# Attention with four PSUM banks for the turned scores, two for the row scores, and the value products between the two row-unit slots of a quad

## The reference, cut to what matters

```python
x = x + _L1_attn_ref(_layernorm(x, axis=-1), ...)
# in _L1_attn_ref: NH, NKV = 32, 8 heads of HD = 16, causal, rotary positions
q = _apply_rope(q, cos, sin)
k = _apply_rope(k, cos, sin)
logits = jnp.einsum('bhqd,bhkd->bhqk', q, k) * scale
logits = jnp.where(causal[None, None], logits, jnp.finfo(logits.dtype).min)
attn = jax.nn.softmax(logits, axis=-1)
out = jnp.einsum('bhqk,bhkd->bhqd', attn, v)
return out.transpose(0, 2, 1, 3).reshape(bsz, q_len, NH * HD) @ Wo.T
```

## Time and profile before

| | us |
|---|---|
| runs shown | 2533.43, 5908.05, 2530.44; median 2533.43 |
| the profiled execution, its own time | 2539.86 |
| its span | 2538.0 |
| granted TensorE clock, mean over the span | 0.958 |

### The profile page before, as it was taken

The page is one execution under the profiler, slowest core; times in us unless marked ns, Lnnn a source line. Parts: engine busy times, 40 slices in busy tenths (PEclk is TensorE's granted clock), DMA queues, the critical chain, the costliest instruction groups (busy, mean ns, idle before and its releaser), DMA issues. The chain is left out here.

```text
span 2538.0 us, 33152 instructions
## 1 busy us (share of the span) xinstructions
PE 2358.7 (93%) x12442; PEld 1812.6 (71%) x12442; DVE 1660.0 (65%) x2163; ACT 1311.4 (52%) x1905; POOL 1330.1 (52%) x876
## 2 busy tenths in 40 slices
PE   6997899999999999999999999999889977877876
PEld 5875788888888888888888888887668744554433
DVE  6555787687687588588588588678365345664414
ACT  3214576577477477477477467567323132234423
POOL 2221498598599499499489589579422200000000
PEclk9998899999999999999999999999889988869988
DMA  5321333233233233233223333232143202000001
GB/s 134 96 73 54 107 113 104 87 110 103 86 102 117 79 112 113 79 108 108 88 92 117 90 102 112 88 100 84 42 116 88 65 14 79 1 2 1 3 1 47
DMA packets 163406, 204.07 MB, mean 80 GB/s; under 512 B 24396, under 2 KB 86224, under 8 KB 163120
## 3 DMA queue, kind: packets, MB, share of 16 engines
q1 hardware_dynamic: 163248, 201.96, 26.5%
HBM read 198.43 MB, written 3.15 MB: 79 GB/s over the span
## 5 line engine op out<-in xcount | busy, mean ns | idle before, releaser
L1914 POOL TENSOR_TENSOR mamba_w_lo<-mamba_raw,mamba_w_hi 128x512 fp32r<-128x512 f32 x272 | 435.8, 1611 | 292.0 <-ACT mamba_w_hi L1742 292.0
L76 PE MATMUL psum<-mamba_hT_lo,mamba_w_hi 128*128 128x512 f32 x1152 | 461.9, 401 | 3.0 <-DVE mamba_bc L2005 3.0
L78 PE MATMUL psum<-mamba_hT_hi,mamba_w_lo 128*128 128x512 f32 x1152 | 456.3, 396 | 0.0
L77 PE MATMUL psum<-mamba_hT_hi,mamba_w_hi 128*128 128x512 f32 x1152 | 456.1, 396 | 0.0
L1933 POOL TENSOR_SCALAR mamba_L<-mamba_A,mamba_ts 128x256 f32<-128x256 f32 (+1 forms) x256 | 335.0, 1322 | 0.1
L2037 DVE TENSOR_TENSOR mamba_L<-mamba_L,mamba_cb 128x1536 f32<-128x1536 f32 x128 | 302.8, 2366 | 22.8 <-ACT mamba_L L1791 14.3
L2005 DVE SCALAR_TENSOR_TENSOR mamba_hid<-psum,mamba_cw,mamba_hid 128x1022 f32<-128x1022 f32 (+2 forms) x192 | 245.1, 1277 | 19.4 <-ACT mamba_hid L1749 14.8
L76 PEld LDWEIGHTS psum<-mamba_hT_lo,mamba_w_hi 128*128 128x128 f32 x1152 | 217.0, 188 | 53.2 <-DVE mamba_bc L2005 3.3
L78 PEld LDWEIGHTS psum<-mamba_hT_hi,mamba_w_lo 128*128 128x128 f32 x1152 | 216.7, 188 | 52.4
L77 PEld LDWEIGHTS psum<-mamba_hT_hi,mamba_w_hi 128*128 128x128 f32 x1152 | 217.1, 188 | 49.1
L2064 DVE SCALAR_TENSOR_TENSOR mamba_zs_lo<-mamba_z,mamba_dgn,mamba_zs_hi 128x512 fp32r<-128x512 f32 x128 | 117.4, 922 | 172.2 <-ACT mamba_zs_hi L1814 172.2
(11 more groups left out here) (281 smaller groups left out, 4945.7 us busy)
## 6 DMA issues: line engine op xcount, KB each, us to landing
mamba_A<-mamba_a_dram SPq DMA_DIRECT2D x128, 512.0 KB, 4.5
mamba_raw<-in_win SPq DMA_DIRECT2D x144, 256.0 KB, 2.6
mamba_raw<-in_wout SPq DMA_DIRECT2D x128, 256.0 KB, 2.6
mamba_Eb<-mamba_e_dram SPq DMA_DIRECT2D x128, 128.0 KB, 3.0
ffn_raw<-in_w SPq DMA_DIRECT2D x80, 128.0 KB, 3.6
ffn_scl<-in_s SPq DMA_DIRECT2D x80, 128.0 KB, 3.7
ffn_scl<-in_s SPq DMA_DIRECT2D x86, 64.0 KB, 2.3
ffn_raw<-in_w SPq DMA_DIRECT2D x20, 256.0 KB, 2.6
```

What stands on the lines that cost most here:

```text
L76: e.matmul(out, wh, ml, start=start, stop=False)
L77: e.matmul(out, wh, mh, start=False, stop=False)
L78: return e.matmul(out, wl, mh, start=False, stop=stop)
L1914: e.tensor_tensor(w.lo[:, k % NSPLIT, :], raw[:, k % NRAW, :], w.hi_read[:, k % NSPLIT, :], ALU.subtract).then_inc(s["w_lo"], 1)
```

## The change

Three things change. Turned scores get four banks, 2 to 5: half m = 0 uses 2 and 3, half m = 1 uses 4 and 5, and `score_t` waits for the exponentials of the half before the last. Row units get one pair, banks 0 and 1: each waits until the reduction of the unit before it is done. And the value products of the quad before move from the end of a quad to its middle, behind the first half's row units and ahead of the second half's `score_t`.

```diff
                 def score(s, z):
                     b, qt = STEPS[s]
                     k, n = s * NQ + z, P * (qt + 1)
-                    if k >= 2:
-                        e.wait_ge(peaked, k - 1)
+                    if k:
+                        e.wait_ge(peaked, k)
                     for h in range(2):
-                        e.matmul(psum[:, 2 * (k % 2) + h, 0:n], qs[HALVES[h], b, z, qt * P:(qt + 1) * P],
+                        e.matmul(psum[:, h, 0:n], qs[HALVES[h], b, z, qt * P:(qt + 1) * P],
                                  ks[HALVES[h], b, 2 * (z // QPK) + h, 0:n], start=True, stop=False)
                     for j in range(2):
                         for h in range(2):
-                            last = e.matmul(psum[:, 2 * (k % 2) + h, n - P:n],
+                            last = e.matmul(psum[:, h, n - P:n],
...
-                    if k:
-                        e.wait_ge(exped, k)
+                    if k >= 4:
+                        e.wait_ge(exped, k - 2)
                     if m == 0 and (j, kt) == (0, 0):
                         e.wait_ge(m_in[s % 2], 64 * (s // 2 + 1))
                     z = QPK * (2 * j + m)
-                    outs = [ps[4 + h].rearrange("p (h q) -> p h q", h=QPK) for h in range(2)]
+                    outs = [ps[2 + k % 4 + h].rearrange("p (h q) -> p h q", h=QPK) for h in range(2)]
...
-                    for m in range(2 if t < TQ else 0):
-                        score_t(t, m)
+                    for m in range(2):
+                        if t < TQ:
+                            score_t(t, m)
                         for k in range(m * len(units) // 2, (m + 1) * len(units) // 2):
                             score(*units[k])
-                    if 1 <= t <= TQ:
-                        weigh(t - 1)
+                        if m == 0 and 1 <= t <= TQ:
+                            weigh(t - 1)
...
-                    e.activation(pt[:, k % NPT, :], ps[4 + k % 2], ACT.Exp, scale=SCALE).then_inc(exped, 1)
+                    e.activation(pt[:, k % NPT, :], ps[2 + k % 4], ACT.Exp, scale=SCALE).then_inc(exped, 1)
...
-                                    psum[:, 2 * (k % 2):2 * (k % 2) + 2, 0:n], AX.X, ALU.max).then_inc(peaked, 1)
+                                    psum[:, 0:2, 0:n], AX.X, ALU.max).then_inc(peaked, 1)
```

## The result

| | before | changed |
|---|---|---|
| median of the runs, us | 2534.66 | 2586.87 |
| lowest and highest run (without 5908.05) | 2530.44, 2535.89 | 2579.02, 2590.72 |
| profiled execution: time, span | 2539.86, 2538.0 | 2579.02, 2577.2 |
| opening, us (clock) | 41.3 (0.56) | 78.1 (0.51) |
| loop to the last output product, us (clock) | 227.8 (0.89) | 233.6 (0.88) |

The ratio of the changed kernel to the one before is 1.0208, 95% interval 1.0175 to 1.0240. The time lies inside the forecast range (2560 to 2593) and 11 us above the forecast. The interval straddles the 2% at which the prediction begins to say "slower", so the runs do not decide between its 76% and its 22%.

What follows compares the result with a forecast made beforehand. DVE's reductions bound the opening; no single engine bounded the loop, where PE waited in turn with others. Opening +36, loop +1, clock +5 made +42 on the 2533.4 us median: 2576 us, 1.7% slower, range 2560 to 2593.

Steps and rivals of the forecast that it cites:

- its 76% and its 22%: Whole kernel: chances given to a time within 2% of before (76%) and to slower by more (22%).
- The opening, +36: Opening's 32 row units: with one pair nothing overlaps, 2.43 us each at half clock, 77 us against 41.3.
- The third rival: Opening stays at full clock: +23 us in place of +36, total 2562 us; chance 5%.
- the 64 of the bound: Opening's lower bound: all units at full clock, 32 x 1.98 + 0.6 = 64 us, +23.
- A plain quad, -0.11: Quad of steps 0 and 1: PE waits 0.79 us for DVE instead of 0.90 for ACT, gaining 0.11.
- Steps 4 and 5, +5.8 at full clock: Loop, two units per half: waits for reductions exceed the exponential waits removed, +0.7 us a quad, 8 quads.
- the 0.4 of the prediction: Loop's clock: each us spent at half clock costs some 0.4 us.
- -4.2, +1.4, +5.8 and -2.4: Loop at full clock: changes in us for steps 0 and 1, 2 and 3, 4 and 5, 6 and 7; together +0.6.
- The turns: Loop: PE waits 1.5 us for ACT's copy, but the next unit's 0.79 wait falls away; net -0.3 to 0.1 each.
- The clock in the loop, +5: Loop: three or four more clock falls, 1.4 us each, in steps 4 and 5; +5, between 0 and 23.
- The second rival: Clock gives way in steps 2 to 5: +23 us in place of +5, total 2593 to 2600 us; chance 15%.
- The first rival: Banks pay in full: all 33.0 us of exponential waits go, reductions hide behind `score_t`; 2531 us, no loss; chance 5%.

Runs made afterwards that it cites:

- e1: Changed kernel, but the opening's row units keep two pairs of banks in turn: 2539.8 us, ratio 1.0040 to the kernel before.
- e4: Changed kernel plus one unread 128x384 filler matmul behind each row unit of the opening: 2567.2 us, ratio 1.0145 to the kernel before.
- e5: Changed kernel with ACT's copy of the results behind a quad's second exponential instead of the fourth: 2570.1 us, ratio 1.0143 to the kernel before.
- e8: Kernel before with a single pair of row-unit banks in the loop, not in the opening: 2565.4 us, ratio 1.0143 to the kernel before.
- e3: Changed kernel with the value products back at the end of a quad: 2586.4 us, ratio 1.0225 to the kernel before.
- e2: Kernel before with the value products moved to the middle of a quad, banks as before: 2513.1 us, ratio 0.9934 to the kernel before.
- e6: e2 with ACT's copy of the results behind the second exponential: 2496.1 us, ratio 0.9852 to the kernel before.
- e9: e6 plus one unread 128x128 filler matmul behind each row unit of the opening: 2501.3 us, ratio 0.9874 to the kernel before.
- e7: Changed kernel with two pairs of banks in the opening and ACT's copy behind the second exponential: 2531.3 us, ratio 0.9991 to the kernel before.

## Why the prediction was right, point by point

- **The opening, +36.** Right. Measured +36.8; a unit 2.44 us for 2.43 forecast; clock 0.51. e1 takes it back whole. The third rival (full clock there) is refuted; e4 shows what it would have been, 64.3 us for the 64 of the bound.
- **A plain quad, -0.11.** Measured 3.44 against 3.45, so 0.0. The wait that replaced the other was right (0.77 for 0.79); the step missed that a row unit takes 0.55 us (2303.07 to 2303.62) instead of 0.44 when PE has stood before it. (Its sum is printed without its first term: 1.13 + 0.44 + 1.00 + 0.34 + 0.44 = 3.35.)
- **Steps 4 and 5, +5.8 at full clock.** They took 22.7 us more. The windows give 0.05 x 2 x 48.4 = 5 us at half before and 0.31 x 2 x 71.1 = 44 after; by the 0.4 of the prediction that is 16 of the 22.7, and 7 are left for the chain. Taken to full clock in the same way the four groups of steps changed by -2.7, +1.3, +6.8 and -3.0 us, together +2.5, where the prediction had -4.2, +1.4, +5.8 and -2.4, together +0.6. So its chains were right group by group, but for the plain quads.
- **The turns.** The wait of 1.5 us was 1.31. That it is given back because PE stands there was wrong: e5 took away 11.1 us of such waits, and its loop at full clock is 11.3 us shorter than the changed kernel's (9.9 us as measured, 16 us by the medians), so nothing of them had been given back. It did not spoil the forecast, since the wait of the next unit does fall away behind a turn, for another reason than the one given.
- **The clock in the loop, +5.** In the traces the loop has 48.8 us at half before and 57.2 after, by the 0.4 about +3: steps 4 and 5 lost 16, the others gained some 13, because the lower clock of the opening ended 5 us sooner in the loop and the last steps swung less. That the two nearly cancel is luck; the prediction had only the falls in steps 4 and 5. The stages around attention, which the sum leaves at nothing, gave -3.4; they had 126 us at half before and 119 after. So the pair of traces gives +39 for the forecast 42.
- **The 11 us above the forecast.** The medians give +52 for 42. The four executions of the changed kernel took 2579.0, 2586.2, 2587.6 and 2590.7 us with mean clocks 0.951, 0.947, 0.948 and 0.946. Time at half is 2 x (1 - clock) x span: 253 us in the fastest and 280 in the slowest, so 27 us more at half for 11.7 us of time, 0.43 for each (the clocks have three digits, so 0.4 to 0.5); in the same way e4's four executions give 0.41 and e8's 0.34. So the time above the forecast goes with more time at half clock, and the clock over the whole program is what the sum has too small. Whether that time lies in the loop is not shown, as one execution in four has a trace; the kernel before spreads by 13 us too. That one trace fits the forecast so closely is in part luck.
- **The page's rule.** The rule that the prediction took from the Trainium skill (TensorE: Matmul & The Clock Gate, "A second HAM failure mode: psum-queue depth-cycling") is that brief idles between groups of matmuls make the clock swing in a kernel that cycles through banks. The trace agrees with it in steps 4 and 5 (0.69), and does not in steps 2 and 3, where PE waits 0.79 and 1.37 us again and again at 1.00.
- **The second rival**, a clock that gives way in steps 2 to 5: it came at a part of its size, in steps 4 and 5 alone. What brings it is the single pair of row banks: e8 is the kernel before with that one edit in the loop, and it is at half in steps 4 and 5 for 39.2 us instead of 4.6. The other traced kernels with it were at half there too (changed 44.4 us, e1 23.9, e3 41.0, e4 13.7, e5 37.5), the others not (e2, e6 and e9 0.0). Each is from one trace. These two lines are steps 4 and 5 of e8 and of e6:

```profile
2384.69:2454.16 69.47, 57.29 (x364) 32.47 (x363) 18.29 (x44) 21.38 (x40) 0.00 (x0) 0.72 0.01 2
...
2351.61:2392.83 41.22, 38.31 (x364) 23.68 (x363) 16.84 (x44) 20.81 (x40) 0.00 (x0) 1.00 0.01 3
```

- **The first rival**, banks that pay in full: refuted by the account of waits (30.3 us new for 33.0 old) and by e7.

Not settled: why the clock falls in one execution of the same loop and not in another. The loops of the changed kernel, e1 and e4 have the same instructions and 57.2, 42.5 and 30.6 us at half; they start in different places and with a different clock, and no run separates the two.

## What to carry to other kernels

In this kernel the second pair of banks did not remove a wait but moved it (33.0 us of old waits, 30.3 of new ones): before one engine gets a second pair of banks at another's cost, write the cycle of both, from start to free again, and compare what each waits for. A wait is cheapest at a place in the program that other work can fill, and moving a product there (e2) can be worth more than doubling a buffer. When work moves up in one engine's program, move what consumes it up in the next engine's program too (e5, e6): in-order engines keep a copy waiting behind work that nobody needs yet.

## What the hardware showed unexpectedly

- More work was faster: a matmul that nobody reads, in each unit's gap, kept the clock at 1.00 and shortened the opening from 78.1 to 64.3 us (e4). In e9 the same trick took 3.0 us off the opening and moved the fall of the clock behind it; no gain shows in the whole time.
- Executions of one kernel differ by what they spend at half clock: e6's four lie within 0.5 us (2495.8 to 2496.3), all at a mean clock of 0.966, the changed kernel's 11.7 us apart (0.951 to 0.946). Idling little does not make a kernel repeat: e9, with e6's loop, spreads 11.7 us as well (2494.0 to 2505.6, clock 0.974 to 0.967).
- One pair of row banks instead of two, and nothing else changed, took the clock in steps 4 and 5 from 0.95 to 0.72 (e8 against before). With the loop body of the change it is 1.00 with the banks of before (e2) and 0.69 with those of the change.
- A row unit of 384 keys costs 0.11 us more when PE has stood idle before it, at full clock: 0.55 instead of 0.44 us.
